# Second experts: W1 and W3 kept whole in SBUF and copied into slots by ScalarE, W2 streamed per tile

## The chip, the cores and the metric

The kernel runs on one core of one Trainium2 chip. The metric is the device time of one execution, in microseconds (us).

## What is computed

A block of two layers acts on x, 2 x 1024 tokens of 256 values in fp32. Each layer adds a gated mixing step and a gated mixture of experts. Only the mixture of layer 1, the "second experts", is touched by the change; attention stands before it.

```python
x = x + tanh(g_xattn[1]) * attention(layernorm(x), context)      # 16 heads, 77 context keys + 1024
h = layernorm(x)
scores = sigmoid(h @ gate_w.T)                                   # 32 experts
top 4 of scores + e_bias per token; weights = their scores / sum of them
g = h @ w1[e]; u = h @ w3[e]                                     # 256 x 192 each
out += weight * ((silu(g) * u) @ w2[e])                          # 192 x 256
x = x + tanh(g_ffn[1]) * out
```

## The kernel before, in words

Each stage is a block of code that gives every engine its own list of instructions (`nc.Block`); all engines meet at the end of a block. Within one, they are ordered by semaphores alone. The stages of layer 1 are `combine_and_project`, `attend`, `project_and_score`, `route`, `experts1` and `combine1`.

`route` sorts the 2048 x 4 (token, expert) pairs by expert and pads them to `NT1` = 95 tiles of 128 rows; a tile has one expert, whose number stands in `e.expert`. `experts1` (L1070 to L1231) then runs over the 95 tiles:

- POOL (`move_tiles`, L896) gathers the 128 rows of a tile by an indirect DMA into one of four slots of `xg`. It needs the column of row numbers that DVE writes (`token_column`, L929).
- SP (`load`, L1103) reads the tile's expert number and loads that expert's W1 and W3, 192 KB each, into one of the four slots of `e.w13` (L1108), once gate and up of four tiles before are done. `store` (L1110) sends the result of the tile six before to `y`.
- TensorE turns the gathered rows (`turn_x`, L1137, two tiles ahead), computes gate and up with the slot's W1 and W3 as the weights that it loads (`gate_up`, L1145), and the product with W2 (`down`, L1155), which lies behind by two tiles. W2 of all 32 experts is in SBUF (`e.w2b`, 64 KB of each partition); `down` picks the tile's by the expert number that it loads into a register (L1150).
- ScalarE does both SiLUs (L1187, L1189), and then copies the turned rows of the tile two ahead from PSUM to SBUF (`copy_x`, L1181).
- DVE multiplies (L1217 to L1219), copies the result of the tile two before into `ysb` (L1205), which waits for the store that last used that slot (L1203), and writes the row numbers of a tile four ahead of the one last turned (L929).

The order within a tile on TensorE is `gate_up(j)`, `down(j - 2)`, `turn_x(j + 2)`. `tile_loop` (L93) writes the first five tiles out and loops over turns of four.

W2 is brought at the end of `attend`: SP, when it has moved the last row maxima of the last group (L1667), issues 16 DMAs (`load_w2`, L1552; four experts in two DMAs: rows 0 to 127 of W2 on 128 partitions, rows 128 to 191 on 64). The pad rows of `e.w2b` are set to zero by POOL early in `attend` (L1737). In `project_and_score` SP stores the 16 normalised tiles to `xn` (L2030), which the gathers read later.

The `arena` of 160 KB of each partition is shared by all stages. Bytes from `ATT0` = 77824 on belong to attention's buffers until `attend` ends.

## Time and profile before

| what | value |
|---|---|
| median of 3 runs | 1368.84 us |
| lowest, highest | 1366.23, 1368.93 us |
| the profiled execution's own time | 1366.11 us |
| its span | 1364.4 us |
| TensorE busy (share of the span) | 1131.3 us (83%) |
| weight loads (PEld) busy | 741.5 us (54%) |
| DVE, ScalarE, POOL busy | 756.2, 585.3, 337.4 us |
| all DMA | 172.77 MB, mean 127 GB/s |

The span goes from the first to the last instruction that the profile shows; 1.7 us of the execution lie outside it. Busy times overlap between engines and don't add up to the span. PE is matmul, PEld is TensorE's weight load, which runs beside it; a name with q (SPq) is an engine's sequencer. "<-" in brackets names what ended an engine's idle time. L numbers are lines of the kernel before.

### The profile page before, as it was taken

Reading aid. Unit: us, or ns where it says so; the run is one execution under the profiler, and the core shown is the slowest. Engines: PE = TensorE matmul, PEld = TensorE weight load, DVE = VectorE, ACT = ScalarE, POOL = GpSimd, SP = SyncE. Lnnn points to the kernel's source line nnn. Section 1 sums busy time; section 2 is a strip of 40 time slices with the busy share of each in tenths; the row PEclk is TensorE's granted clock in tenths of the full one; section 3 lists DMA queues with packets and bytes.
Section 4 is the critical chain, followed back from the end, with each engine's and each line's share of the span. In section 5 each row is a group of like instructions: output and inputs, shape, how many; then the busy total and the mean of one; then the engine's idle time right before and its main releaser. Section 6 shows DMA issues by size and latency. Waiting matters only on the chain. (4 is left out here: it accounts for less than half of the span.)

```text
span 1364.4 us, 24973 instructions
## 1 busy us (share of the span) xinstructions
PE 1131.3 (83%) x6984; PEld 741.5 (54%) x6986; DVE 756.2 (55%) x2072; ACT 585.3 (43%) x1394; POOL 337.4 (25%) x538
## 2 busy tenths in 40 slices
PE   4849999999957879999999999997547999999200
PEld 2749999999944412333333333324417999888200
DVE  6551222222236487888888888832594555555433
ACT  2631221222124406777777777785453333333000
POOL 2012222222211244111111101010003333333476
PEclk9959999999978958999999999999658999999755
DMA  5455555554523533213113123043107888899343
GB/s 165 141 192 194 190 171 178 188 185 169 177 73 95 113 95 49 34 17 50 27 24 50 20 31 50 1 112 86 51 1 224 259 259 258 258 263 254 110 131 119
DMA packets 139935, 172.77 MB, mean 127 GB/s; under 512 B 17574, under 2 KB 118944, under 8 KB 139738
## 3 DMA queue, kind: packets, MB, share of 16 engines
q1 hardware_dynamic: 126186, 138.75, 37.7%
q0 software_dynamic: 11376, 31.08, 7.6%
q10 hardware_dynamic: 2304, 2.10, 0.4%
q8 instruction: 34, 0.56, 0.2%
q14 instruction: 35, 0.29, 0.1%
HBM read 141.29 MB, written 30.38 MB: 126 GB/s over the span
## 5 line engine op out<-in xcount | busy, mean ns | idle before, releaser
L1932 DVE TENSOR_REDUCE arena<-ps 128x1 f32<-128x512 f32 x512 | 327.7, 682 | 60.9 <-PE ps L1773 57.5
L1903 ACT ACTIVATE arena<-ps 128x512 f32<-128x512 f32 (+1 forms) x576 | 301.8, 598 | 130.4 <-PE ps L1814 129.0
L1814 PE MATMUL ps<-arena 99*128 99x512 bf16 (+1 forms) x576 | 216.6, 388 | 3.1 <-ACT arena L1903 2.7
L1773 PE MATMUL ps<-arena 96*128 96x512 bf16 x512 | 206.0, 405 | 8.8 <-PEq L1349 6.1
L896 POOL DMA_INDIRECT xg<-xn,tcol x134 | 127.7, 953 | 335.7 <-DVE tcol L929 332.6
L1803 PE MATMUL ps<-arena 128*17 128x512 f32 (+1 forms) x1152 | 153.3, 604 | 2.1 <-ACT arena L1903 1.0
L1814 PEld LDWEIGHTS ps<-arena 99*128 99x128 bf16 (+1 forms) x576 | 57.1, 101 | 174.5 <-ACT arena L1903 136.1
L987 PEld LDWEIGHTS ps<-scratch,arena 128*128 128x128 f32 x1248 | 147.4, 194 | 3.6 <-issue 1.7
L987 PE MATMUL ps<-scratch,arena 128*128 128x128 f32 x1248 | 147.9, 278 | 1.1 <-ACT scratch L1018 1.1
L1145 PE MATMUL ps<-scratch,arena 128*128 128x128 f32 x1140 | 146.4, 279 | 1.7 <-DMA arena<-in_L_ffn_w 0.5
L1000 PE MATMUL ps<-arena,scratch 128*128 x624 | 141.0, 379 | 0.0
L1145 PEld LDWEIGHTS ps<-scratch,arena 128*128 128x128 f32 x1140 | 135.9, 193 | 5.6 <-issue 4.2
L1000 PEld LDWEIGHTS ps<-arena,scratch 128*128 128x128 f32 x624 | 115.8, 190 | 14.0
L1057 DVE TENSOR_SCALAR scratch<-ps,arena 128x128 f32<-128x128 f32 x156 | 43.9, 344 | 126.4 <-PE ps L987 126.4
L1018 ACT ACTIVATE scratch<-ps 128x256 f32<-128x256 f32 x39 | 14.9, 383 | 209.5 <-PE ps L978 209.5
L1155 PE MATMUL ps<-arena,scratch 128*128 (+1 forms) x380 | 97.9, 380 | 0.7 <-DVE ysb L1205 0.7
L1217 DVE TENSOR_TENSOR scratch<-ps,scratch 64x128 f32<-64x128 f32 x95 | 27.8, 293 | 109.2 <-PE ps L1155 104.2
L1773 PEld LDWEIGHTS ps<-arena 96*128 96x128 bf16 x512 | 51.4, 101 | 58.7 <-DVE arena L1932 26.3
L1721 POOL TENSOR_TENSOR scratch<-arena 128x64 f32<-128x64 f32 x64 | 18.7, 292 | 255.0 <-DVE arena L1951 246.5
L1181 ACT ACTIVATE scratch<-ps 128x256 f32<-128x256 f32 x95 | 36.4, 383 | 86.8 <-PE ps L1137 86.8
L1251 POOL DMA_INDIRECT arena<-y,slot_u x64 | 61.2, 957 | 36.4 <-issue 19.2
L1155 PEld LDWEIGHTS ps<-arena,scratch 128*128 128x128 f32 (+1 forms) x380 | 65.3, 192 | 6.0 <-issue 1.1
(306 smaller groups left out, 1262.9 us busy)
## 6 DMA issues: line engine op xcount, KB each, us to landing
arena<-in_L_ffn_W SPq DMA_DIRECT2D x47, 1024.0 KB, 5.0
arena<-in_L_ffn_w SPq DMA_DIRECT2D x190, 192.0 KB, 3.7
y<-ysb SPq DMA_DIRECT2D x95, 128.0 KB, 4.2
arena<-k_parts SPq DMA_DIRECT2D x48, 137.6 KB, 5.0
arena<-q_parts SPq DMA_DIRECT2D x96, 64.0 KB, 6.0
arena<-y SPq DMA_DIRECT2D x16, 256.0 KB, 5.5
arena<-in_L_ffn_w SPq DMA_DIRECT2D x8, 512.0 KB, 10.3
xg<-xn,tcol POOLq DMA_INDIRECT x134, 4.4
```

Source lines behind the costliest of these rows:

```text
L896: pool.indirect_dma_start(out=e.xg[:, r, :], out_offset=None, in_=e.xn[layer], in_offset=bass.IndirectOffsetOnAxis(ap=e.tcol[:, r:r + 1], ...
L987: ins = nc.tensor.matmul(chunk(r, n), w1[:, r % 2, k, n * P:(n + 1) * P], xT[:, r % 2, k, :], start=(k == 0), stop=(k == DK - 1))
L1000: last = nc.tensor.matmul(ps[:, YB + r % 2, 0:D], hT[:, r % 2, k, :], e.w2[:, ex, k, :], start=(k == 0), stop=(k == HK0 - 1))
L1057: v.tensor_scalar(hT[:, r % 2, k, :], chunk(r, k), e.b1T[:, bass.ds(ex * HK0 + k, 1)], 0.0, ALU.add, ALU.max).then_inc(high_ready, 1)
L1145: ins = nc.tensor.matmul(chunk(r, n), e.w13[:, r, k, n * P:(n + 1) * P], xT[:, r % 2, k, :], start=(k == 0), stop=(k == DK - 1))
L1155: last = nc.tensor.matmul(ps[:, YB + r % 2, 0:D], hT[0:rows, r % 2, k, :], e.w2b[0:rows, ex, k, :], start=(k == 0), stop=(k == 1))
L1251: pool.indirect_dma_start(out=yg[:, i, k, :], out_offset=None, in_=e.y[1], in_offset=bass.IndirectOffsetOnAxis(ap=e.slot_u[:, i, k:k + 1], ...
L1773: nc.tensor.matmul(ps[:, MAXB + pos % NMAXB, :], e.q_aug[u][0:QROWS, c, h, t * P:(t + 1) * P], e.k_aug[u][0:QROWS, h, CL + k * HB:CL + (k ...
L1803: ins = nc.tensor.matmul(ps[h * 32:h * 32 + HD + 1, AB, :], e.v_g[u][0:rows, mt, h, :], e.prob[s % 2][0:rows, h, :], start=(mt == 0), stop ...
L1814: nc.tensor.matmul(ps[0:rows, SB + n % NSB, :], e.k_aug[u][0:AROWS, h, k0:k0 + rows], e.q_aug[u][0:AROWS, c, h, :], start=True, stop=True) ...
L1903: nc.scalar.activation(e.prob[s % 2][0:rows, h, :], ps[0:rows, SB + (s * GH + h) % NSB, :], ACT.Exp).then_inc(p_ready, 1)
L1932: v.tensor_reduce(e.mx[:, c, h, t, k:k + 1], ps[:, MAXB + pos % NMAXB, :], AX.X, ALU.max).then_inc(max_done, 1)
```

## The change

W2_1 and W13_1 change roles. W1 and W3 of all 32 experts (3072 bytes of each partition per expert) lie in SBUF whole, at the arena's start. Of these, 25 experts fit below `ATT0` and are loaded by SP at the end of `attend` in 50 DMAs of 192 KB; the other 7 are loaded by SP at the start of `project_and_score`, 14 DMAs, ahead of the stores to `xn`. In `experts1` ScalarE reads the tile's expert number and copies that expert's 768 fp32 values of each partition from the whole array into one of four slots (`bring`), and `gate_up` reads the slot. SP streams W2 per tile instead, into four slots (`e.w2r`), in two DMAs of 128 KB and 64 KB; each waits for the `down` of four tiles before. `down` waits for its W2 and no longer loads the expert number. The zeroing of the pad rows moves from POOL in `attend` to DVE at the start of `experts1`. The number of matmuls, their shapes and their order stay.

```diff
--- before.py
+++ after.py
@@ -51,9 +51,9 @@
 RAW0 = 2 * DK * H0 * 4
 ARENA0_END = W2_0 + E0 * HK0 * D * 4
 W13_BYTES = DK * 2 * I1 * 4
-W2_1 = 0
-W13_1 = W2_1 + E1 * 2 * D * 4
-W2_TURN = 4
+W13_1 = 0
+W13_RING = W13_1 + E1 * W13_BYTES
+W2_1 = W13_RING + RING1 * W13_BYTES
 ARENA = 163840
 ZN_AT = 32768
 YG0 = 32768
@@ -61,7 +61,8 @@
 LOGITS_AT = 3 * 4 * D * 4
 TOP = ARENA - (DK * D + D + DK * E1) * 4
 LOGITS1_AT = TOP - NTILE * E1 * 4
-ATT0 = W13_1 + RING1 * W13_BYTES
+ATT0 = 77824
+W13_EARLY = (ATT0 - W13_1) // W13_BYTES
 IA, IB = P, I1 - P
 IB_PAD = 96
 
@@ -134,7 +135,7 @@
         return e.used[-1]
 
     e.sem = new_semaphore
-    e.w0_in, e.w2_in = (ctx.enter_context(nc.semaphore(n)) for n in ("w0_in", "w2_in"))
+    e.w0_in, e.w13_in = (ctx.enter_context(nc.semaphore(n)) for n in ("w0_in", "w13_in"))
     e.x = sb("x_resident", [P, NTILE, D])
     e.arena = sb("arena", [P, ARENA // 4])
     e.scr = sb("scratch", [P, NTILE * D])
@@ -197,8 +198,9 @@
     e.w1 = carve(W1_0, [2, DK, H0])
     e.w2 = carve(W2_0, [E0, HK0, D])
 
-    e.w2b = carve(W2_1, [E1, 2, D])
-    e.w13 = carve(W13_1, [RING1, DK, 2 * I1])
+    e.w13 = carve(W13_1, [E1, DK * 2 * I1])
+    e.w13r = carve(W13_RING, [RING1, DK, 2 * I1])
+    e.w2r = carve(W2_1, [RING1, 2, D])
 
     e.raw = Memory()
     e.raw.wqkv = carve(RAW0, [6, D])
@@ -1071,8 +1073,8 @@
 
     nc, ps, sem = e.nc, e.ps, e.sem
     gathered = [sem(f"e1_gathered{r}") for r in range(RING1)]
-    w13_in = [sem(f"e1_w13_in{r}") for r in range(RING1)]
-    x_turned, xT_ready = sem("e1_x_turned"), sem("e1_xT_ready")
+    w2_in = [sem(f"e1_w2_in{r}") for r in range(RING1)]
+    x_turned, xT_ready, w13_ready = sem("e1_x_turned"), sem("e1_xT_ready"), sem("e1_w13_ready")
     gu_raw, silu_ready, h_ready = sem("e1_gu_raw"), sem("e1_silu_ready"), sem("e1_h_ready")
     y_raw, y_ready, tcol_ready = sem("e1_y_raw"), sem("e1_y_ready"), sem("e1_tcol_ready")
     y_stored = [sem(f"e1_y_stored{r}") for r in range(RING1)]
@@ -1103,9 +1105,10 @@
             def load(j, r):
                 ex = sp.value_load(e.expert[0:1, bass.ds(j, 1)], min_val=0, max_val=E1 - 1)
                 if at_least(j, RING1):
-                    sp.wait_ge(gu_raw, (j - RING1) * 2 + 2)
-                for at, name in ((0, "L1_ffn_w1"), (I1, "L1_ffn_w3")):
-                    sp.dma_start(e.w13[:, r, :, at:at + I1], e.a[name][bass.ds(ex, 1)].rearrange("e (k p) i -> p (e k) i", p=P)).then_inc(w13_in[r], 16)
+                    sp.wait_ge(y_raw, j - RING1 + 1)
+                w = e.a["L1_ffn_w2"][bass.ds(ex, 1)]
+                sp.dma_start(e.w2r[0:IA, r, 0, :], w[:, 0:IA].rearrange("e p d -> p (e d)")).then_inc(w2_in[r], 16)
+                sp.dma_start(e.w2r[0:IB, r, 1, :], w[:, IA:I1].rearrange("e p d -> p (e d)")).then_inc(w2_in[r], 16)
 
             def store(j, r):
                 sp.wait_ge(y_ready, j + 1)
@@ -1138,31 +1141,29 @@
                 last.then_inc(x_turned, 1)
 
             def gate_up(j, r, turn):
-                pe.wait_ge(w13_in[r], turn * 32 + 32)
+                pe.wait_ge(w13_ready, j + 1)
                 pe.wait_ge(xT_ready, j + 1)
                 for n in range(3):
                     for k in range(DK):
-                        ins = nc.tensor.matmul(chunk(r, n), e.w13[:, r, k, n * P:(n + 1) * P], xT[:, r % 2, k, :], start=(k == 0), stop=(k == DK - 1))
+                        ins = nc.tensor.matmul(chunk(r, n), e.w13r[:, r, k, n * P:(n + 1) * P], xT[:, r % 2, k, :], start=(k == 0), stop=(k == DK - 1))
                     if n != 1:
                         ins.then_inc(gu_raw, 1)
 
-            def down(j, r):
-                ex = pe.value_load(e.expert[0:1, bass.ds(j, 1)], min_val=0, max_val=E1 - 1)
+            def down(j, r, turn):
                 if at_least(j, 2):
                     pe.wait_ge(y_ready, j - 1)
                 pe.wait_ge(h_ready, j + 1)
+                pe.wait_ge(w2_in[r], turn * 32 + 32)
                 for k, rows in enumerate((IA, IB_PAD)):
-                    last = nc.tensor.matmul(ps[:, YB + r % 2, 0:D], hT[0:rows, r % 2, k, :], e.w2b[0:rows, ex, k, :], start=(k == 0), stop=(k == 1))
+                    last = nc.tensor.matmul(ps[:, YB + r % 2, 0:D], hT[0:rows, r % 2, k, :], e.w2r[0:rows, r, k, :], start=(k == 0), stop=(k == 1))
                 last.then_inc(y_raw, 1)
 
             def body(j, r, turn, first, last):
                 if at_least(j, 2):
                     pe.wait_ge(h_ready, j - 1)
                 gate_up(j, r, turn)
-                if isinstance(j, int) and j == 2:
-                    pe.wait_ge(e.w2_in, 32 * (E1 // W2_TURN))
                 if at_least(j, 2):
-                    down(j - 2, (r - 2) % RING1)
+                    down(j - 2, (r - 2) % RING1, turn if r >= 2 else turn - 1)
                 if before(j, NT1 - 2):
                     turn_x(j + 2, (r + 2) % RING1, turn + (r + 2) // RING1)
 
@@ -1170,7 +1171,7 @@
                 turn_x(j, j, 0)
             tile_loop(pe, NT1, RING1, body)
             for j in (NT1 - 2, NT1 - 1):
-                down(j, j % RING1)
+                down(j, j % RING1, j // RING1)
 
         @block.scalar
         def _(act):
@@ -1179,6 +1180,12 @@
                 if at_least(j, 2):
                     act.wait_ge(gu_raw, (j - 2) * 2 + 2)
                 nc.scalar.activation(xT[:, r % 2].rearrange("p k t -> p (k t)"), ps[:, XB + r % 2, 0:D], ACT.Copy).then_inc(xT_ready, 1)
+
+            def bring(j, r):
+                ex = act.value_load(e.expert[0:1, bass.ds(j, 1)], min_val=0, max_val=E1 - 1)
+                if at_least(j, RING1):
+                    act.wait_ge(gu_raw, (j - RING1) * 2 + 2)
+                nc.scalar.activation(e.w13r[:, r].rearrange("p k i -> p (k i)"), e.w13[:, ex, :], ACT.Copy).then_inc(w13_ready, 1)
 
             def body(j, r, turn, first, last):
                 if at_least(j, 2):
@@ -1189,8 +1196,11 @@
                 nc.scalar.activation(silu[0:IB, r % 2, 1, :], chunk(r, 1)[0:IB], ACT.Silu).then_inc(silu_ready, 1)
                 if before(j, NT1 - 2):
                     copy_x(j + 2, (r + 2) % RING1)
-
+                    bring(j + 2, (r + 2) % RING1)
+
+            act.wait_ge(e.w13_in, 32 * E1)
             for j in range(2):
+                bring(j, j)
                 copy_x(j, j)
             tile_loop(act, NT1, RING1, body)
 
@@ -1225,6 +1235,7 @@
             for j in range(RING1):
                 token_column(e, dve, j, j, tcol_ready)
             v.memset(hT[IB:IB_PAD, :, 1, :], 0.0)
+            v.memset(e.w2r[IB:IB_PAD, :, 1, :], 0.0)
             next_column(0, 0)
             tile_loop(dve, NT1, RING1, body)
             for j in (NT1 - 2, NT1 - 1):
@@ -1549,10 +1560,9 @@
         sp.dma_start(e.q_aug[u][n * HD:(n + 1) * HD, 1, :, :], qv[cq, gg, :, :, bass.ds(b * S + HB, HB)]).then_inc(e.q2_loaded[u], 16)
 
 
-def load_w2(e, eng, ex):
-    w = e.a["L1_ffn_w2"][ex:ex + W2_TURN]
-    eng.dma_start(e.w2b[0:IA, ex:ex + W2_TURN, 0, :], w[:, 0:IA].rearrange("e p d -> p e d")).then_inc(e.w2_in, 16)
-    eng.dma_start(e.w2b[0:IB, ex:ex + W2_TURN, 1, :], w[:, IA:I1].rearrange("e p d -> p e d")).then_inc(e.w2_in, 16)
+def load_w13(e, eng, ex):
+    for at, name in ((0, "L1_ffn_w1"), (I1, "L1_ffn_w3")):
+        eng.dma_start(e.w13[:, ex].rearrange("p (k i) -> p k i", k=DK)[:, :, at:at + I1], e.a[name][ex].rearrange("(k p) i -> p k i", p=P)).then_inc(e.w13_in, 16)
 
 
 STEPS = 2 * MT
@@ -1580,7 +1590,7 @@
     rows_max, neg_ready, negT_ready = sem("at_rows_max"), sem("at_neg_ready"), sem("at_negT_ready")
     step, carrier = sem("at_step"), sem("at_carrier")
     s_raw, p_ready, pv_done = sem("at_s_raw"), sem("at_p_ready"), sem("at_pv_done")
-    bias_added, pad_set = sem("at_bias_added"), sem("at_pad_set")
+    bias_added = sem("at_bias_added")
     half_out, half_inverted, half_done = (sem("at_half_" + n) for n in ("out", "inverted", "done"))
     MAXB, NMAXB, SB, NSB, AB, MB = 0, 3, 3, 3, 6, 7
     PARTS = len(QB)
@@ -1681,8 +1691,8 @@
                     maxima(g + 1, 1 - u, 0)
 
             groups(sp, body)
-            for ex in range(0, E1, W2_TURN):
-                load_w2(e, sp, ex)
+            for ex in range(W13_EARLY):
+                load_w13(e, sp, ex)
 
         @block.gpsimd
         def _(pool):
@@ -1734,8 +1744,6 @@
                 last = g_.tensor_tensor(e.x[:, i, :], e.x[:, i, :], e.bproj, ALU.add)
             last.then_inc(bias_added, 1)
             pool.wait_ge(bias_added, 1)
-            g_.memset(e.w2b[IB:IB_PAD, :, 1, :], 0.0).then_inc(pad_set, 1)
-            pool.wait_ge(pad_set, 1)
 
             def body(g, u, first, last):
                 if not last:
@@ -2025,6 +2033,8 @@
     with nc.Block() as block:
         @block.sync
         def _(sp):
+            for ex in range(W13_EARLY, E1):
+                load_w13(e, sp, ex)
             for i in range(NTILE):
                 sp.wait_ge(zn_ready, i + 1)
                 sp.dma_start(e.xn[1][i * P:(i + 1) * P, :], zn[:, i, :]).then_inc(zn_stored, 16)
```

## Rows read from the trace of the kernel before

**Rows 1.** Stretches of 30 us (its first line names the columns).

```profile
core 0: us, PE busy (x) PEld busy (x) DVE busy (x) ACT busy (x) POOL busy (x), PEclk, DMA share, GB/s
...
1050.00:1080.00 30.00, 30.00 (x222) 28.00 (x221) 16.25 (x60) 11.44 (x37) 10.95 (x12) 1.00 0.88 256
...
1200.00:1230.00 30.00, 29.40 (x213) 26.62 (x212) 15.65 (x59) 10.80 (x35) 11.20 (x12) 1.00 0.91 265
```

**Rows 2.** Timeline of one steady tile: start us, us, engine, line, what.

```profile
1152.85 0.89 SPq L1108 DMA_DIRECT2D arena<-in_L_ffn_w  x2
1152.88 0.38 PE L1137 MATMUL ps<-ident,xg 128*128 128x128 f32 x2
1152.91 0.94 POOL L896 DMA_INDIRECT xg<-xn,tcol  x1 [1.89 <-DVE tcol L929]
...
1153.10 1.50 PE L1145 MATMUL ps<-scratch,arena 128*128 128x128 f32 x12
...
1153.30 0.38 ACT L1181 ACTIVATE scratch<-ps 128x256 f32<-128x256 f32 x1 [0.82 <-PE ps L1137]
...
1154.64 0.27 ACT L1189 ACTIVATE scratch<-ps 64x128 f32<-64x128 f32 x1 [0.62 <-PE ps L1145]
...
1155.53 0.66 PE L1145 MATMUL ps<-scratch,arena 128*128 128x128 f32 x4
1155.58 0.29 DVE L1217 TENSOR_TENSOR scratch<-ps,scratch 64x128 f32<-64x128 f32 x1 [1.02 <-PE ps L1155]
```

**Rows 3.** Timeline of the second experts, its start and its last turned tile.

```profile
1029.46 0.15 DVE L929 COPY tcol<-token_u 128x1 uint32<-128x1 uint32 x1 [4.82 <-PE ps L1137]
...
1030.41 0.69 PE L1137 MATMUL ps<-ident,xg 128*128 128x128 f32 x2 [0.98 <-DMA xg<-xn,tcol]
...
1265.45 0.44 PE L1137 MATMUL ps<-ident,xg 128*128 128x128 f32 x2 [0.46 <-DMA xg<-xn,tcol]
```

**Rows 4.** Waits, 1033 to 1276 us: who waited for whom, us, times, longest.

```profile
PEld ps L1137 <- DMA xg<-xn,tcol: 4.5, 7, 1.4
PEld ps L1145 <- issue: 4.2, 13, 0.6
```

**Rows 5.** DMA issues, 1060 to 1260 us: KB each, median us to landing.

```profile
y<-ysb SPq DMA_DIRECT2D x79, 128.0 KB, 4.3
xg<-xn,tcol POOLq DMA_INDIRECT x80, 4.5
```

**Rows 6.** DMA of the first experts, 80 to 380 us.

```profile
DMA packets 15544, 53.08 MB, mean 177 GB/s; under 512 B 1871, under 2 KB 3023, under 8 KB 15407
...
xg<-xn,tcol POOLq DMA_INDIRECT x39, 3.4
```

**Rows 7.** ScalarE: line 741, and the timeline behind a loaded register.

```profile
L741 ACT ACTIVATE arena<-arena x1: 629/629/629, 977.5 to 977.5; 128x512 f32<-128x512 f32 x1
...
253.32 1.14 ACT L1028 ACTIVATE scratch<-ps,arena 128x128 f32<-128x128 f32 x4 [0.50 <-issue]
```

**Rows 8.** SP's DMA issues in attend, timeline, and that block's closing drain.

```profile
903.89 0.58 SPq L1554 DMA_DIRECT2D arena<-in_L_ffn_w  x1
...
923.45 2.29 SPq L1555 DMA_DIRECT2D arena<-in_L_ffn_w  x1
949.13 10.18 SPq L2030 DMA_DIRECT2D xn<-scratch  x7
...
L1660 POOLq DRAIN  x1: 386/386/386, 937.5 to 937.5; - x1
```

**Rows 9.** DMA queue of SP: 900 to 940 us, then 1024 to 1040 us.

```profile
q1 hardware_dynamic: 6496, 6.30, 72.0%
...
q1 hardware_dynamic: 3333, 2.41, 52.6%
```

**Rows 10.** Timeline of POOL at the start of attend.

```profile
517.73 6.92 POOL L1737 MEMSET arena<- 32x8192 f32 x1
...
535.31 0.26 POOL L1710 TENSOR_SCALAR arena<-arena 128x16 f32<-128x16 f32 x1 [7.15 <-DVE arena L1944]
```

## The prediction

> **What bounds the kernel now.** I first read the page's slices for the stretch that the change touches, the second experts, then a table by stretches of 30 us [rows 1]. There TensorE is busy for 98 to 100% at full clock, its weight loads for 89 to 93%, the DMA engines for 88 to 91% at some 260 GB/s, ScalarE for little over a third. Two things are near their limit, so I went on to the timeline of a steady tile [rows 2]: gate and up start at 1153.10 and again at 1155.53, a period of 2.43 us, in which one weight load follows another without a gap. That is TensorE's own rate, and the change leaves its matmuls alone. Were every tile like this, DMA would cost nothing. So I compared with the whole stretch: tile 1 is turned at 1030.41, the last at 1265.45 [rows 3], 93 periods in 235.04 us, 2.527 us each. **The excess is 93 x 0.097 = 9.0 us.** The waits name it [rows 4]: weight loads stood idle 4.5 us for gathered rows, and 4.2 us ahead of gate and up for what the profile calls issue, in 13 places; this kernel's only other wait there is that for the tile's W1 and W3. Both are DMAs that come a little late.
>
> **Why gathers are late, and what relieves them.** In a steady tile POOL starts a gather at 1152.91, as a tile is turned; its own tile is turned two periods after that, 4.83 us later [rows 2]. The median gather lands after 4.5 us here [rows 5], so the slow part of them misses. In the first experts, at 177 GB/s, it lands after 3.4 us [rows 6]. A tile moves 384 KB of weights, a gather and a store of 128 KB each. With W2 (192 KB) in place of W1 and W3 it moves 448 KB rather than 640 KB, in 2.43 us 189 GB/s, near the rate of the first experts. I take their latency: 1.4 us to spare. Bounds: the 4.5 us of today (no gain) and 3.4 us with no stall left (9.0 us). Since single gathers will still be late, I leave 0.7 us. Gain: **8.3 us**. The wait of gate and up for W1 and W3 goes from DMA to ScalarE, below.
>
> **What is added to ScalarE.** Per tile: a register load with its checks, and a copy of 128x768 fp32 within SBUF. The nearest copy is 128x512 fp32 from arena to arena, 0.63 us; a 128x256 from PSUM takes 0.38 [rows 7, 2], so 256 more cost some 0.21 to 0.25 us, and the copy 0.84 to 0.88 us. The register load is seen in the first experts, in the same order of work: there line 1028 follows the copy of the turned rows and a load of the expert number, and starts after 0.50 us of issue [rows 7]. Hence in the steady tile: copy of turned rows 1153.30 to 1153.68, copy of weights 1154.18 to about 1155.02. Its tile's gate and up start at 1155.53 [rows 2], so 0.5 us is left. ScalarE's whole round is 0.38 + 0.50 + 0.84 + two SiLUs of 0.27 = 2.26 us of 2.43. The SiLU of the next tile waits behind the copy: the second one, now at 1154.64, comes at about 1155.3 and ends before 1155.58, when DVE starts on its product after waiting for `down` [rows 2]. The cover for all of this is TensorE's 2.43 us. I cost it at 0.2 us for the first tiles, which have no `down` and a shorter period. If a copy took over 0.17 us more than I think, ScalarE would set the period.
>
> **SP in the second experts.** Two DMAs per tile before and after, 0.89 us of issue at 1152.85 [rows 2]. The load's wait moves to `down` of four tiles before, and the store of the tile six before is queued behind it. So that store leaves about 1.0 us after a `down` ends and lands 4.3 us later at today's latency [rows 5], 5.3 us after. DVE wants its slot two periods and the three products (0.9 us) after that `down`, 5.8 us after. It holds by 0.5 us today and by more with lighter traffic; if it failed, DVE's copy, then the row numbers queued behind it, then the gather would be late. Cost 0. W2 is asked for at `down` of four tiles before, four periods (9.7 us) ahead of its use: 0.
>
> **The start.** The zeroing of four slots' pad rows on DVE is hidden: DVE idles 4.82 us there until the first rows are turned [rows 3]. The first gathers compete with 0.8 MB of W2 rather than 1.6 MB, so they may land up to 0.9 us earlier: 0.5 us gained. POOL's zeroing of 6.92 us leaves `attend`, but POOL idles 7.15 us after it until 535.31 [rows 10], so it gains 0. The register load on TensorE's queue is hidden behind weight loads: 0.
>
> **The loads moved ahead.** SP issues the W2 DMAs from 903.89 to 925.74 [rows 8], and POOL reaches the block's end at 937.5: 11.8 us to spare. Now SP has 50 DMAs with 25 x 512 = 12,800 packets of 768 B instead of 6144 of 1 KB. Two rows price a packet of SP's queue [rows 9]: in 900 to 940 us 72.0% of 16 x 40 us over 6496 packets is 71 ns; in 1024 to 1040 us 52.6% of 16 x 16 us over 3333 is 40 ns, and these are mostly the very transfers that now move, W1 and W3, same shape, same source. I take 40 ns: 12,800 x 40 / 16 = 32 us, all landed at about 937, and SP done with issuing some us before that, since the queue holds what the engines have not taken (its last DMA before, issued at 923.45, was in the queue after 925.74). It waits for nobody. Cost 0. At 71 ns it costs 18 us (below).
>
> The Trainium skill, "SBUF — State Buffer", section "Door 1: The DMA port swizzle", says that a transfer reaches only as many of 16 ports as its partitions map to, and partitions 0 to 63 map to eight. Half of the W2 DMAs have 64 partitions, those of W1 and W3 all 128; by this rule 71 ns belongs to W2 and not to the loads that come. The sum is the same without it.
>
> The last 14 DMAs stand ahead of the `xn` stores on SP. 14 x 0.45 us of issue from 938 end at 944, landed by about 947; the first store leaves at 949.13 [rows 8]. Cost 0.
>
> **Sum.** -8.3 - 0.5 + 0.2 = -8.6 us. It is made against the profiled execution, 1366.11 us, 2.7 us below the median of 1368.84. From the median: **1360.2 us**.
>
> **Rivals.**
> *SP holds the end of `attend` (slower).* All engines wait for the slowest queue at the block's end. SP's issue is throttled to what the engines take. At 71 ns a packet, the first 6144 go in 21.85 us as now and the other 6656 at 4.44 ns each in 29.5 us: SP is done at 955.3 rather than 937.5, +17.8 us, 1378 us in all. It decides above some 49 ns: about 11,000 packets, the rest still queued, in the 33.6 us up to 937.5. At 53 ns (71 scaled to 768 B) it costs 3 us: 1363. For it: attention's own rows were the ones with 71 ns. Against: the same transfers at 40 ns. 0.06 for the first, 0.12 for the second.
> The Trainium skill, "DMA: Bandwidth & Descriptors", section "Bandwidth", speaks against the smaller DMAs: batch to 1 MiB or more; alone, 64 KB reaches 138 GB/s there. By that figure, an estimate, 9.8 MB would take 71 us and hold the block's end by over 25 us; the trace has 260 GB/s with DMAs of 128 to 192 KB, so it does not agree for queued ones.
> *ScalarE sets the period.* Were the copy 1.1 us or more, the round would be 2.52 us: +0.09 x 95 = 8.6 us, which gives everything back: 1368.8, and 9.5 us more per further 0.1 us. For it: only 0.17 us of slack, and register steps that the page doesn't count as busy. Against: the rows for both its parts. 0.12.
> *Gathers stay late.* If their 4.5 us is the gather's own and not the traffic's, only the waits for W1 and W3 go (4.2 us at most, perhaps 1): 1365 to 1368. Against: 3.4 us in the first experts. 0.10.
> The forecast has 0.60.
>
> **How the numbers follow.** About 0.2%, 2.7 us, is what a measurement of this kernel can tell from no change. Faster by more: the forecast, the small hold of `attend` and a part of the two last rivals, 0.76. Slower: the full hold and a ScalarE copy of 1.15 us or more, 0.12. Between: 0.12. The range goes down to 1355 (all 9.0 and 0.9 us gained and the profiled execution's 2.7 us lower level, with 1 us to spare) and up to 1369, which takes in the small hold, late gathers and the ScalarE round of 2.52 us; the full hold is left out.
>
> **What would show it.** Right: periods of 2.43 us nearly throughout, 93 of them in about 227 us; no wait of weight loads for gathered rows over 1 us in sum; gathers landing in about 3.4 us and 190 GB/s; ScalarE's copy 0.84 us and ending half a us ahead of gate and up; the drain of SP at the end of `attend` before POOL's; `xn` stores at the same distance from the block's start. Wrong: weight loads idle for ScalarE's copy in most tiles; TensorE's first work of `project_and_score` released by SP; DVE's copy into `ysb` waiting for stores.

## The result, and the profile after

The median went from 1368.84 us (five runs, 1366.23 to 1371.49) to **1378.84 us** (five runs, 1376.61 to 1381.63): 1.0078 of before, with a 95% interval of 1.0055 to 1.0100. The forecast was 1360.2 us, so the change costs 10.0 us where 8.6 were to be gained. The profiled execution took 1381.63 us with a span of 1379.9 us, 15.5 us over the span of before. It is the slowest of its five, and that of before (1366.11 us) is faster than all its other runs, so that 5.5 of the 15.5 us come from which executions were profiled.

I start where the forecast has its sum, at the turned tiles. Timeline of TensorE in after, tile 1 and the last tile (start us, us, engine, line, what):

```profile
1032.38 0.69 PE L1140 MATMUL ps<-ident,xg 128*128 128x128 f32 x2 [0.75 <-DMA xg<-xn,tcol]
...
1279.79 0.44 PE L1140 MATMUL ps<-ident,xg 128*128 128x128 f32 x2
```

That is 247.41 us for 93 periods, 2.660 us each, where [rows 3] gave 235.04 us and 2.527. So **12.4 of the 15.5 us lie in the second experts**. The other 3.1 us are the sum of four steps: 1.8 us more up to the end of `attend`, 1.2 from there to TensorE's last instruction of `route`, 1.2 behind the last turned tile, and 1.0 less between `route` and the turn of tile 1. The first two are not shown to be the change's: in the kernels of the experiments below, `attend` ends between 937.5 and 940.3 us, whichever loads it issues, and `route` is done 85.4 or 86.6 to 86.7 us later. Stretches of 30 us in after, answering to [rows 1]:

```profile
core 0: us, PE busy (x) PEld busy (x) DVE busy (x) ACT busy (x) POOL busy (x), PEclk, DMA share, GB/s
1050.00:1080.00 30.00, 30.00 (x224) 27.95 (x223) 15.78 (x58) 19.05 (x51) 11.37 (x12) 1.00 0.59 171
1200.00:1230.00 30.00, 28.21 (x196) 24.11 (x194) 14.91 (x55) 17.00 (x44) 10.42 (x11) 1.00 0.57 169
```

In the first stretch TensorE runs as before, with nothing between its matmuls. Later it does 196 matmuls in 30 us rather than 213. DMA is not what it lacks: the share fell from 0.88 to 0.59. Nor is it ScalarE, busy for 17 to 19 of 30 us. No engine of the table is near its limit in the second stretch, so the next view is that of the waits, 1036 to 1290 us of after:

```profile
POOL xg L898 <- DVE tcol L931: 157.5, 90, 3.7
DVE ysb L1215 <- DMA y<-ysb: 99.0, 81, 2.1
...
PEld ps L1140 <- DMA xg<-xn,tcol: 20.3, 46, 1.2
...
PEld ps L1148 <- issue: 5.3, 14, 0.5
```

The second row is new: DVE stands 99 us in sum for stores of `y`. The third is what TensorE feels of it, and the fourth, 5.3 us of "issue" ahead of gate and up, is taken up in "Why the prediction was wrong". DVE's copy into `ysb` waits for a slot that a store has not yet emptied; the row numbers are queued behind it on DVE; POOL's gather waits for them; and TensorE waits for the gather. It is the chain that the prediction named under "SP in the second experts", where it set it against 0.5 us of slack with stores that land after 4.3 us. But the stores land faster than before, not slower. DMA issues in after, 1060 to 1260 us, answering to [rows 5]:

```profile
DMA packets 30932, 34.14 MB, mean 171 GB/s; under 512 B 4765, under 2 KB 28546, under 8 KB 30932
...
y<-ysb SPq DMA_DIRECT2D x74, 128.0 KB, 2.2
```

2.2 us from issue to landing. So the stores are issued late, and SP is who issues them. What does SP wait for? Its own waits, first in before (1036 to 1262 us), then in after (1036 to 1290 us):

```profile
SPq L1112 <- DVE ysb L1205: 0.4, 1, 0.4
```

```profile
SPq L1110 <- PE ps L1158: 7.4, 3, 6.3
SPq L1115 <- DVE ysb L1215: 1.4, 3, 0.9
```

**SP waits for nothing, in either kernel.** The 7.4 us in after lie ahead of its first store. A queue that waits for nothing over 90 tiles has no time left, and the profile's page has no column that would say so, because it doesn't count such instructions as busy. Stores of `y` on SP, timeline, before and then after:

```profile
1050.29 0.37 SPq L1112 DMA_DIRECT2D y<-ysb  x1
...
1260.04 0.37 SPq L1112 DMA_DIRECT2D y<-ysb  x1
```

```profile
1050.72 0.37 SPq L1115 DMA_DIRECT2D y<-ysb  x1
...
1260.07 0.42 SPq L1115 DMA_DIRECT2D y<-ysb  x1
```

In before 83 rounds lie between the two stores, 2.527 us each, the period of TensorE. In after there are 78, **2.684 us each**. Other first and last stores of the same stretch give 2.53 to 2.54 and 2.68 to 2.70 us, so the third decimal is no evidence. Where a round goes, from the views of SP's lines: duration in ns, lowest/median/highest, of one instruction of each kind; first before, then after.

```profile
L1104 SPq FUSED_REGOPS  x161: 46/152/177, 1024.2 to 1260.9; - x161
L1104 SPq TENSOR_LOAD <-expert x95: 262/270/739, 1023.9 to 1260.6; - x95
...
L1108 SPq DMA_DIRECT2D arena<-in_L_ffn_w x190: 372/394/1495, 1024.7 to 1261.8; - x190
L1108 SPq FUSED_REGOPS  x95: 37/43/48, 1024.5 to 1261.2; - x95
...
L1112 SPq DMA_DIRECT2D y<-ysb x95: 332/368/1505, 1039.2 to 1273.7; - x95
L1112 SPq FUSED_REGOPS  x88: 46/46/51, 1039.1 to 1259.9; - x88
```

```profile
L1106 SPq FUSED_REGOPS  x161: 51/155/171, 1027.2 to 1282.6; - x161
L1106 SPq TENSOR_LOAD <-expert x95: 262/270/662, 1026.9 to 1282.3; - x95
...
L1110 SPq FUSED_REGOPS  x95: 37/43/43, 1027.5 to 1282.9; - x95
...
L1110 SPq DMA_DIRECT2D arena<-in_L_ffn_w x95: 337/341/357, 1027.7 to 1283.0; - x95
...
L1111 SPq FUSED_REGOPS  x95: 37/43/47, 1028.1 to 1283.4; - x95
...
L1111 SPq DMA_DIRECT2D arena<-in_L_ffn_w x95: 479/503/1390, 1028.2 to 1283.9; - x95
...
L1115 SPq DMA_DIRECT2D y<-ysb x95: 332/418/562, 1047.2 to 1288.6; - x95
L1115 SPq FUSED_REGOPS  x88: 51/51/56, 1047.1 to 1281.5; - x88
```

With three register moves of 29 ns and a check of 18 ns in each kernel, one of each kind, taken at its median, adds up to 1.772 us before (270 + 152 + 18, 43 + 2 x 29 + 2 x 394, 46 + 29 + 368) and 1.929 us after (270 + 155 + 18, 43 + 29 + 341, 43 + 29 + 503, 51 + 29 + 418). The difference is 0.157 us, as is that of the two rounds; that they agree to the thousandth is luck. Its parts: the second DMA, of 64 partitions, takes 503 ns where one of W1 or W3 takes 394 (+0.109); the first takes 341 (-0.053); the second DMA has register steps of its own (+0.043); the store's issue takes 418 ns rather than 368 (+0.050, and 0.008 in register steps, of which 0.003 are the load's). The change has two DMAs for two, fewer bytes, and a longer round.

The rest of the round, 0.75 us, is not in this sum of medians. Summed over all rows of SP in those rounds, the loop's own and the slower ones among the shown included, SP's instructions take 1.95 us a round before and 2.09 after. The last 0.57 and 0.60 us are in no row: waits that were already fulfilled and steps between instructions. Timeline of SP in after, which shows a turn of the loop:

```profile
1149.79 0.42 SPq L1115 DMA_DIRECT2D y<-ysb  x1
1151.07 0.34 SPq L1110 DMA_DIRECT2D arena<-in_L_ffn_w  x1
1151.61 0.50 SPq L1111 DMA_DIRECT2D arena<-in_L_ffn_w  x1
1152.30 0.43 SPq L1115 DMA_DIRECT2D y<-ysb  x1
1154.11 0.34 SPq L1110 DMA_DIRECT2D arena<-in_L_ffn_w  x1
```

From the end of one store to the next load's first DMA it takes 0.86 us (1150.21 to 1151.07), from the next store's end 1.38 us (1152.73 to 1154.11). This longer gap comes once in four tiles, which is once in a turn of the loop. The rounds of after are three of 2.50 to 2.59 us and one of 2.9 to 3.3 (3.14 in the median); those of before three of 2.38 to 2.6 and one of 2.7 to 3.2 (2.90).

The Trainium skill, "Perfetto Trace Analysis", section "What "DMA-bound" means", says that a kernel can be bound by the sequencer that issues DMAs, and that one sees it by a track of solid DMA slices. The first half is what happened here. The second would have missed it: DMA slices fill 0.341 + 0.503 + 0.418 = 1.26 us of a round of 2.68 in after, 47%. The section "Sequencer-only Instruction (DRAIN, etc)" of the same page says that waits on semaphores and their propagation are outside the reported window; the 0.57 to 0.60 us without a row agree with that, though no run here splits them.

### The profile page after: what moved, and what is told of

It is laid out like the page before. It is cut to its first block and busy times, and to the rows that moved or that the text cites. A ratio compares the mean times of both kernels' runs of the same rounds, so it can differ in the third digit from the quotient of the medians.

```text
span 1379.9 us, 25229 instructions
## 1 busy us (share of the span) xinstructions
PE 1142.5 (83%) x6985; PEld 740.8 (54%) x6986; DVE 757.5 (55%) x2073; ACT 645.7 (47%) x1489; POOL 330.7 (24%) x537
## 5 line engine op out<-in xcount | busy, mean ns | idle before, releaser
L1020 ACT ACTIVATE scratch<-ps 128x256 f32<-128x256 f32 x39 | 15.0, 384 | 209.9 <-PE ps L980 209.9
L1158 PE MATMUL ps<-arena,scratch 128*128 128x256 f32 (+1 forms) x380 | 98.5, 382 | 1.5 <-DVE ysb L1215 1.3
L1188 ACT ACTIVATE arena<-arena 128x768 f32 x95 | 80.1, 843 | 41.4 <-PE ps L1148 34.2
L1215 DVE COPY ysb<-ps 128x256 f32<-128x256 f32 x95 | 40.4, 425 | 100.2 <-DMA y<-ysb 99.0
```

What stands on the lines that cost most here:

```text
L1158: last = nc.tensor.matmul(ps[:, YB + r % 2, 0:D], hT[0:rows, r % 2, k, :], e.w2r[0:rows, r, k, :], start=(k == 0), stop=(k == 1))
L1188: nc.scalar.activation(e.w13r[:, r].rearrange("p k i -> p (k i)"), e.w13[:, ex, :], ACT.Copy).then_inc(w13_ready, 1)
```

## The experiments

**Theory S:** SP's own instructions set the period, 2.53 us before and 2.68 after, and TensorE's 2.43 comes back once SP's round is shorter. **Rivals:** ScalarE's copy sets it (C); the order of load and store on SP does, with a store held behind a load that waits for `down` (O); the DMA traffic does (D), which the prediction held for the kernel before. All stretches below go from the turn of tile 1 to that of the last tile, in each kernel's profile; before has 235.0 us, after 247.4.

| run | stretch, us | period, us | time, us | before beside it, us | ratio (95%) |
|---|---|---|---|---|---|
| e1 after, SP written out | 227.1 | 2.442 | 1356.66 | 1368.02 | 0.9903 (0.9886 to 0.9919) |
| e2 before, SP written out | 235.8 | 2.535 | 1365.47 | 1368.02 | 0.9974 (0.9959 to 0.9988) |
| e3 after, store ahead of load | 240.2 | 2.583 | 1373.70 | 1368.02 | 1.0041 (1.0026 to 1.0057) |
| e4 after, a third of the copy | 245.1 | 2.636 | 1380.19 | 1368.02 | one run |
| e5 before, one more register load | 284.2 | 3.056 | 1417.75 | 1364.73 | one run |
| e6 after, second DMA on 128 partitions | 228.3 | 2.454 | 1361.62 | 1364.73 | 0.9978 (0.9969 to 0.9988) |
| e7 before written out, without W3 | 226.8 | 2.438 | 1357.56 | 1364.73 | 0.9943 (0.9926 to 0.9959) |
| e8 after, one W2 DMA | 226.9 | 2.439 | 1361.15 | 1364.73 | one run |
| e9 after, W2's rest at partition 64 | 257.9 | 2.773 | 1393.68 | 1368.07 | 1.0183 (1.0169 to 1.0197) |
| e10 as e1, another chip | 226.9 | 2.440 | 1360.60 | 1368.07 | 0.9945 (0.9932 to 0.9959) |
| e11 e9 with SP written out | 257.8 | 2.772 | 1390.43 | 1368.07 | 1.0166 (1.0150 to 1.0181) |
| e12 e1 with one more register load | 274.3 | 2.950 | 1409.53 | 1368.07 | one run |
| e13 as e9, full-height weights | 230.1 | 2.474 | 1365.32 | 1368.60 | 0.9977 (0.9964 to 0.9990) |

### SP's list written out (e1, e2, e10)

In both kernels the loop on SP's queue becomes 89 bodies one after another; nothing else is touched. It takes the loop's turn and the register steps of computed addresses off SP.

```diff
-            turns = (NT1 - LAG_Y) // RING1
-            with sp.Fori(0, turns) as t:
-                for u in range(RING1):
-                    body(t * RING1 + (LAG_Y + u), (LAG_Y + u) % RING1, None, False, False)
-            for j in range(LAG_Y + turns * RING1, NT1):
+            for j in range(LAG_Y, NT1):
                 body(j, j % RING1, None, False, False)
```

> The changed kernel, with SP's list for the second experts written out for all 95 tiles in place of a loop over turns of four: wait values, slots and addresses of the stores become constants and the branch goes; the loads, stores, waits and their order stay. Theory S (SP's own instructions, 2.69 us a tile, set the period): SP's round falls by 0.3 us or more to under 2.43, the mean period falls from 2.65 to about 2.45 us, and the kernel gains about 95 x 0.2 = 19 us, to some 1360 us; DVE's waits for stores (99 us) nearly vanish. Theory O (the store is late because it is queued behind a load that waits for a down product): DVE's waits for stores stay, and the time stays within 5 us of 1379. Theory C (ScalarE's copy of 0.84 us is in the way): no change.

> The kernel before, with SP's list for the second experts written out in the same way. Theory S: SP's round of 2.53 us was the bound already, so its mean period falls from 2.53 towards 2.43, up to 9 us gained; what is left over 2.43 is late DMA. Theory G (in the kernel before only DMA traffic made gathers and weights late, as I predicted): no change, 1369 us, and the waits for gathered rows stay at 4.5 us.

**Measured.** e1: 1356.66 us, 0.9903 of before. Timeline of TensorE in e1, tile 1 and the last tile:

```profile
1030.77 0.69 PE L1136 MATMUL ps<-ident,xg 128*128 128x128 f32 x2 [0.88 <-DMA xg<-xn,tcol]
...
1257.89 0.38 PE L1136 MATMUL ps<-ident,xg 128*128 128x128 f32 x2
```

Its stretch is 227.1 us, the "93 of them in about 227 us" of the prediction. SP now waits; its waits in e1, 1036 to 1262 us:

```profile
SPq L1115 <- DVE ysb L1211: 7.9, 28, 1.0
SPq L1110 <- PE ps L1154: 7.7, 3, 6.4
```

The waits of the other engines in e1 have neither DVE's row for stores (99.0 us in after) nor one of TensorE for gathers. e2: 1365.47 us, 0.9974 of before, while its stretch shows nothing gained (its profile is of an execution of 1369.32 us, at the upper end of its ten runs). SP waits 40.0 us there for results that are not ready, so it isn't the bound, and yet a period is 2.535 us. The waits of SP and of TensorE in e2, same stretch:

```profile
SPq L1112 <- DVE ysb L1201: 40.0, 78, 1.2
...
PEld ps L1133 <- DMA xg<-xn,tcol: 6.2, 18, 1.0
...
PEld ps L1141 <- issue: 4.8, 13, 0.5
```

**What follows.** In after SP's round is the whole of the loss in the second experts: the same data moved by the same DMAs, with SP's queue freed of its loop, gains what was forecast. In before two limits lie together near 2.53 us: SP's round, and late DMAs behind it. Taking SP away from before leaves the second almost untouched.

The same kernel on another chip, with which the later runs are compared:

> The changed kernel with SP's list written out, once more for its interval: 1356.7 us within 2, period 2.44 us, ratio to the kernel before 0.990 to 0.995.

**Measured.** 1360.60 us, above the 1356.7 within 2 that I expected, and 0.9945 of before, inside the expected ratio; the period is 2.440 us again. The gain in time differs between the chips, 11.4 and 7.5 us, by more than the intervals allow; the stretch of the second experts doesn't (227.1 and 226.9 us). So what differs lies outside it: in the two profiles `attend` ends at 937.5 and 939.5 us, a difference that kernels with either set of loads show. No run here says what sets it.

### The order on SP, and ScalarE's copy (e3, e4)

e3 puts the store ahead of the load:

```diff
             def body(j, r, turn, first, last):
-                load(j, r)
                 if at_least(j, LAG_Y):
                     store(j - LAG_Y, (r - LAG_Y) % RING1)
+                load(j, r)
```

> The changed kernel, with each tile's store issued ahead of the load instead of behind it, so that no store is queued behind a wait for a down product. Theory S: SP's round is the same 2.69 us, so the period stays 2.65 and the time 1379 within 3 us; the late wait may move from the slot of the result to another place. Theory O: DVE's waits for stores vanish and the period falls to about 2.45 us, 1360 us.

e4 lets ScalarE copy 256 of the 768 values of each partition:

```diff
-                nc.scalar.activation(e.w13r[:, r].rearrange("p k i -> p (k i)"), e.w13[:, ex, :], ACT.Copy).then_inc(w13_ready, 1)
+                nc.scalar.activation(e.w13r[:, r].rearrange("p k i -> p (k i)")[:, 0:256], e.w13[:, ex, 0:256], ACT.Copy).then_inc(w13_ready, 1)
```

> The changed kernel, with ScalarE copying only the first 256 of the 768 values of each partition, so that gate and up work on wrong weights: part of the copy is left out. ScalarE is relieved of some 0.42 us a tile. Theory C: the period falls by 0.1 to 0.2 us, 10 to 19 us in all. Theories S and O: no change, 1379 us within 3.

**Measured.** e3: 1373.70 us, 5 us under after and outside what either theory expected, 2.637 us a round of SP over 80 rounds, still without a wait behind its first tiles. The order is worth more than I had put it at. Part of it is S's own: the queue stays full, and its round is 0.05 us shorter. The rest, I take it, is who gets the lateness, which no run shows by itself: DVE's wait for stores fell to 45.2 us, and `down` waits for W2 in its place (7.6 us, and 8.0 us of "issue"). Rival O in its own words, a store held behind a load that waits for `down`, falls by the waits of after: in steady tiles SP's load waits for nothing. e4, whose gate and up work on weights that are in part wrong: 1380.19 us, 1.3 us over the median of after, 2.3 us less in the stretch, with SP's round at 2.68 us and DVE's wait for stores still at 82.9 us (to 1262 us; 89.4 in after). A copy takes 0.417 us there. **C falls**: with two thirds of the copy gone the loss stays, but for those 2.3 us.

### Doses on SP's queue (e5, e12)

One register load per tile whose value nobody uses, in before and in e1's kernel:

```diff
             def load(j, r):
+                sp.value_load(e.expert[0:1, bass.ds(j, 1)], min_val=0, max_val=E1 - 1)
                 ex = sp.value_load(e.expert[0:1, bass.ds(j, 1)], min_val=0, max_val=E1 - 1)
```

> The kernel before, with the expert number loaded into a register once more per tile on SP, to no use: some 0.27 us of load, 0.15 and 0.02 us of check and the gaps between them, about 0.5 us in all; no DMA is added. Theory S: SP's round of 2.53 us has no slack, so it becomes 3.0 us and the time rises by 95 x 0.5 = 47 us, to some 1415 us. If TensorE or DMA were the bound before (2.43 us of TensorE, DMA as it is), most of the 0.5 us would still show, since 2.53 + 0.5 is over 2.43, but only if SP is full already; with SP as idle as I took it to be, nothing would show.

> The changed kernel with SP's list written out, and with the expert number loaded once more per tile on SP, to no use (about 0.5 us). Written out, SP's instructions take some 2.38 us of 2.43, of which 0.58 us is the issue of the store, which was 0.42 us in the loop. If that is SP's own fixed cost, the round becomes 2.85 us and the time rises by 95 x 0.42 = 40 us to some 1397. If part of the issue time is a wait for room in the queue, that SP spends either way, the rise is smaller, down to 0.25 us a tile, 24 us, to 1380.

**Measured.** e5: 1417.75 us, as expected under S; the stretch grew by 49.1 us, 0.528 us per tile. The added load with its steps shows 0.274 + 0.152 + 0.018 = 0.444 us in the view of its line. So the whole of it came through, and 0.084 us that no row has. SP has no slack in the kernel before. e12: 47.2 us over e1's stretch, 0.508 us per tile, and again all of it, in a kernel that gave TensorE 2.44 us. I had left some room there, and 1409.53 us is above my range of 1380 to 1397. SP's round in e1's kernel is thus just under TensorE's period (most rounds take 2.38 us), and no more: the store's issue takes 583 ns there (418 in after), which eats a part of what the written-out list saves.

### W2's second DMA (e6, e8)

e6 moves rows 64 to 191 to 128 partitions in place of rows 128 to 191 to 64: twice the bytes. e8 leaves the DMA out.

```diff
-                sp.dma_start(e.w2r[0:IB, r, 1, :], w[:, IA:I1].rearrange("e p d -> p (e d)")).then_inc(w2_in[r], 16)
+                sp.dma_start(e.w2r[0:P, r, 1, :], w[:, I1 - P:I1].rearrange("e p d -> p (e d)")).then_inc(w2_in[r], 16)
...
-            v.memset(e.w2r[IB:IB_PAD, :, 1, :], 0.0)
```

```diff
-                sp.dma_start(e.w2r[0:IB, r, 1, :], w[:, IA:I1].rearrange("e p d -> p (e d)")).then_inc(w2_in[r], 16)
...
-                pe.wait_ge(w2_in[r], turn * 32 + 32)
+                pe.wait_ge(w2_in[r], turn * 16 + 16)
```

> The changed kernel, with the second W2 DMA of a tile taking 128 rows (64 to 191) onto 128 partitions instead of 64 rows onto 64: the second half of the down product gets wrong rows. More bytes (512 KB a tile for 448), same number of DMAs. In the changed kernel SP spends 0.50 us on issuing the 64-partition DMA and 0.34 us on the 128-partition one. Theory S with the 64-partition shape as the dear part: the issue falls to 0.34 us, SP's round from 2.69 to about 2.52 us, the time by 10 to 15 us, to 1364 to 1369 us, in spite of the added bytes. If bytes in flight set SP's issue time, it stays at 0.50 us or more and the time at 1379 or above.

> The changed kernel, loop as it is, with the second W2 DMA of a tile left out (rows 128 to 191 of W2 are never loaded). SP saves 0.50 us of issue and about 0.12 us of register steps: its round would be 2.07 us, under TensorE's 2.43. Theory S: the period is 2.43 to 2.45 us and the time 1357 us within 3, as with the list written out. Theory C or O: still over 1370 us.

**Measured.** The view of line 1111 in e6:

```profile
L1111 SPq DMA_DIRECT2D arena<-in_L_ffn_w x95: 332/333/358, 1028.8 to 1262.5; - x95
```

**The DMA with twice the bytes is issued in 0.333 us rather than 0.503.** SP's round falls to 2.438 us over 86 rounds, though the loop is kept, TensorE's period to 2.454 us, and the time to 1361.62 us, 0.9978 of before. I had expected a round of about 2.52 us and 1364 to 1369 us; the time is below that, on a chip where before takes 4 us less than in the result. The round falls by 0.25 us, of which this DMA is 0.170; the store's issue is at 0.35 to 0.36 us rather than 0.42, another 0.06. In e8 the period is 2.439 us, as expected, and SP now waits:

```profile
SPq L1110 <- PE ps L1157: 54.2, 72, 9.2
```

So taking the instruction away gives TensorE little more than making it short (2.439 and 2.454 us a tile). The time of e8's one run, 1361.15 us, is 1 us above my range of 1357 within 3; in its profile `attend` ends 2.7 us later than in e1's.

### What traffic is worth (e7)

Before with SP's list written out, and W3 not loaded:

```diff
-                for at, name in ((0, "L1_ffn_w1"), (I1, "L1_ffn_w3")):
+                for at, name in ((0, "L1_ffn_w1"),):
...
-                pe.wait_ge(w13_in[r], turn * 32 + 32)
+                pe.wait_ge(w13_in[r], turn * 16 + 16)
```

> The kernel before with SP's list written out, and with W3 not loaded: up works on what lies in the slots. The traffic of a tile falls from 640 to 448 KB, that of the changed kernel, without ScalarE's copy and without W1 and W3 ahead of time. Theory: in the kernel before two limits lay close together, SP's round and late gathers under 260 GB/s; with SP written out the second is left (6.2 us of waits for gathered rows, period 2.535). If it is the traffic, gathers now land in about 3.4 us, the period is 2.43 to 2.45 us as in the changed kernel written out, and the time 1357 us within 3. If gathers are late for another reason, the period stays at 2.53 and the time at 1365.

**Measured.** 1357.56 us, 0.9943 of before. Timeline of TensorE in e7, tile 1 and the last tile:

```profile
1033.58 0.69 PE L1133 MATMUL ps<-ident,xg 128*128 128x128 f32 x2 [0.99 <-DMA xg<-xn,tcol]
...
1260.34 0.38 PE L1133 MATMUL ps<-ident,xg 128*128 128x128 f32 x2
```

The period is 2.438 us; W1 lands in 2.5 us and `y` in 2.0. e2 and e7 both have SP written out and waiting; what differs is one DMA of 192 KB per tile, and that takes 2.535 down to 2.438 us. So D is right as a second limit of before, worth 9 us of the stretch, and it is this one that the change removes.

### W2 on all 128 partitions, with the whole computation (e9, e11, e13)

e6 shows the price of 64 partitions but multiplies other rows than the layer wants. e9 keeps the short DMA and puts the rest in order: rows 64 to 191 fill the slot's 128 partitions, of which 64 to 127 hold the wanted rows; the second half of the SiLU and of the product moves to partitions 64 to 127, and `down` takes its second part from there. e11 is e9 with SP's list written out.

```diff
...
-                for k, rows in enumerate((IA, IB_PAD)):
-                    last = nc.tensor.matmul(ps[:, YB + r % 2, 0:D], hT[0:rows, r % 2, k, :], e.w2r[0:rows, r, k, :], start=(k == 0), stop=(k == 1))
+                for k, first in enumerate((0, P - IB)):
+                    last = nc.tensor.matmul(ps[:, YB + r % 2, 0:D], hT[first:P, r % 2, k, :], e.w2r[first:P, r, k, :], start=(k == 0), stop=(k == 1))
...
-                nc.scalar.activation(silu[0:IB, r % 2, 1, :], chunk(r, 1)[0:IB], ACT.Silu).then_inc(silu_ready, 1)
+                nc.scalar.activation(silu[IB:P, r % 2, 1, :], chunk(r, 1)[0:IB], ACT.Silu).then_inc(silu_ready, 1)
...
```

> The changed kernel, loop as it is, whole computation: the second W2 DMA takes rows 64 to 191 onto 128 partitions, so that rows 128 to 191 lie on partitions 64 to 127, and the second half of the SiLU, of the products and of the down product is kept on those partitions (64 rows, no pad). As in the run with the same DMA and wrong rows, SP's issue of it is 0.33 us instead of 0.50, its round some 2.44 us, and the time 1361 us within 3, at least 12 us under the changed kernel and some 3 us under the kernel before. If moving half the work to the upper partitions costs TensorE, DVE or ScalarE anything, the steady period is over 2.43 us.

> Both: SP's list written out and W2's second DMA on 128 partitions. SP gets 0.15 us more to spare, but TensorE's 2.43 us is reached already, so theory S expects nothing more: 1356 to 1359 us. The added bytes (512 KB a tile for 448) could make single gathers late and cost 1 or 2 us.

**Measured.** 1393.68 and 1390.43 us, where I had expected 1361 within 3 and 1356 to 1359. Both are slower than after, by the same 10.4 us of the stretch. SP's list makes no difference to the period (2.773, 2.772), so this is not SP. Timeline of a steady tile in e9:

```profile
1152.37 0.29 PEld L1158 LDWEIGHTS ps<-arena,scratch 64*128 64x128 f32 x2 [0.33 <-issue]
...
1152.99 0.20 PEld L1140 LDWEIGHTS ps<-ident,xg 128*128 128x128 f32 x2 [0.33 <-issue]
```

Two gaps of 0.33 us in every tile, one ahead of the weight load of 64 rows and one behind it, in which TensorE waits for nothing that the profile shows. The matmuls in flight cover a part of them; what is left is 2.77 less 2.43, 0.34 us a tile. e13 keeps all of e9 but lets the second part of `down` take 128 rows, with zeros in the lower 64 rows of `hT`:

```diff
-                for k, first in enumerate((0, P - IB)):
-                    last = nc.tensor.matmul(ps[:, YB + r % 2, 0:D], hT[first:P, r % 2, k, :], e.w2r[first:P, r, k, :], start=(k == 0), stop=(k == 1))
+                for k in range(2):
+                    last = nc.tensor.matmul(ps[:, YB + r % 2, 0:D], hT[:, r % 2, k, :], e.w2r[:, r, k, :], start=(k == 0), stop=(k == 1))
...
+            v.memset(hT[0:P - IB, :, 1, :], 0.0)
```

> The changed kernel, loop as it is, whole computation: W2's second DMA takes rows 64 to 191 onto 128 partitions as in e9, but the second half of the down product takes all 128 partitions, with zeros in the SiLU product's lower 64, so that no matmul has its weights on partitions 64 to 127 alone. The SiLU and the product stay shifted to the upper partitions as in e9. In e9 the period was 2.77 us, with gaps of 0.33 us ahead of the 64-row weight load and ahead of the next one. If the gaps come from the weights on the upper 64 partitions alone: they vanish, SP's round of 2.44 us with its 0.33 us issue is left, and the time is 1361 us within 3. If they come from the shifted SiLU or product: the period stays at 2.77 us and the time at 1393.

**Measured.** 1365.32 us (twelve runs), 0.9977 of before, 1.3 us above the range that I expected; the stretch is 230.1 us. Timeline of TensorE's weight loads in e13, the four of `down` and the next:

```profile
1150.74 0.73 PEld L1158 LDWEIGHTS ps<-arena,scratch 128*128 128x128 f32 x4
1151.50 0.36 PEld L1140 LDWEIGHTS ps<-ident,xg 128*128 128x128 f32 x2
```

The gaps of 0.33 us are gone. So they belong to the weight load that takes 64 rows from partition 64 on, and not to the shifted SiLU and product. Whether the number of rows or the place does it was not tried; a load of 96 rows from partition 0 (before and after have it in every tile) shows no such gap. For 64 rows of zeros e13 is 28.4 us faster than e9 by the medians, and 13.5 us faster than after, with the loop kept. It doesn't reach e1: SP's mean round over 84 rounds is 2.486 us rather than the 2.44 that I expected, and DVE still waits 14.0 us for stores.

**The best version** of these is e1: the change, with SP's list written out. On two chips it was faster than before (0.9903 and 0.9945); beside after it was not run, but lies 22 and 18 us under its 1378.84 us.

## Why the prediction was wrong

**The step that failed** is "SP in the second experts", with its "Two DMAs per tile before and after, 0.89 us of issue" and "Cost 0". It counted a queue by its DMAs. SP's round is 2.53 us, of which the 0.89 us are a third, and the new round was never added up. It measured 2.684 us, 0.157 longer than before; against TensorE's 2.43 us, 0.25 us a tile are missing. The first 20 or so tiles run at 2.43 us, since SP enters its loop ahead; then the lead is used up. The price: 247.4 us for the stretch against the 227 forecast.

**The reading of the kernel before** was half right. "TensorE's own rate" and "the excess" of 9.0 us stand nearly: 93 periods of 2.43 are 226.0 us, and e1, e7, e8 and e10 all end at 226.8 to 227.1, so that 7.9 to 8.3 us of the 9.0 could be had. But "Both are DMAs that come a little late" asked only why they land late, not when they were asked for. e5 shows that SP had no time left, e2 that the traffic binds too: with SP freed it alone gives 2.535 us. That SP alone would give 2.53 is read from its missing waits; no run took the traffic away and left SP's round. The row that says so, 0.4 us of waits of SP over 90 tiles, was in the trace of before, and the prediction doesn't have it among its rows. It also took the 4.2 us of "issue" ahead of gate and up for waits for W1 and W3, as the only other wait there. In the code gate and up wait for the turned rows and the SiLU product too, and after, which loads no W1 or W3 there, has the same row with 5.3 us in 14 places; e1 and e7 have none. So this row is not shown to be those loads.

**Relief of the gathers, -8.3 us:** right in mechanism and in size, once SP is out of the way. DMA went from 256 GB/s to 186 in e1 (1050 to 1080 us; 190 forecast), gathers no longer hold TensorE there, and the stretch fell by 7.9 us (235.0 to 227.1). The forecast landing of a gather, 3.4 us, is not shown: the views of after, e1 and e7 give no time for it.

**ScalarE:** right. The view of line 1188 in after:

```profile
L1188 ACT ACTIVATE arena<-arena x95: 842/843/845, 1027.5 to 1281.1; 128x768 f32 x95
```

0.843 us against "0.84 to 0.88", and e4 shows that a copy half as long gives 2.3 us of the 20.3 that after lacks. In a steady tile of e1 the copy ends at 1092.14 and gate and up start at 1092.78, 0.64 us later, where the prediction left 0.5. The nearest rows [rows 7] carried it. The rival "ScalarE sets the period" is refuted in after, and in e1 too, where the full copy runs at a period of 2.442 us. The Trainium skill, "ScalarE: Activation LUTs", section "What ACT_TABLE_LOAD costs", has a rule for an activation with immediate scale and bias, 186 ns and 0.833 ns for each element of a partition. By it, an estimate, 768 take 826 ns; the trace agrees to 2%.

**The wait that the change adds** was named and priced by the wrong quantity. "It holds by 0.5 us" took landing at 4.3 us and a store issued as soon as the load's wait ends. Landing was 2.2 us, so the slack by this sum was 2.6 us. The store was late because SP got to it late. The place was right, DVE's copy into `ysb`, and my last line of what would show the prediction wrong names it; the cause that I would have read into it, a load holding the store, is not it: in steady tiles SP's load waits for nothing.

**The loads moved ahead** cost nothing, as forecast. Timeline of SP at the end of `attend` in after, its next stage, the drains that close the block, and SP's queue from 905 to 940 us (packets, MB, share of 16 engines' time):

```profile
905.71 41.22 SPq L1565 DMA_DIRECT2D arena<-in_L_ffn_w  x64
952.43 2.86 SPq L2040 DMA_DIRECT2D xn<-scratch  x3
...
L1670 SPq DRAIN  x1: 122/122/122, 934.6 to 934.6; - x1
...
L1670 POOLq DRAIN  x1: 386/386/386, 939.3 to 939.3; - x1
...
q1 hardware_dynamic: 13696, 9.85, 93.9%
```

SP reaches the end at 934.6 us and POOL at 939.3. The price of 40 ns a packet held: 93.9% of 16 x 35 us over 13,696 packets is 38 ns. I had put SP's issue at "some us before" 937; the rival "SP holds the end of `attend`" would need it behind POOL's. The 14 later DMAs end at 946.9, ahead of the first store at 952.43, which waits for data. That store stands 13.1 us behind POOL's drain, 11.6 in before; e2, e5 and e7, with the loads of before, have 13.2 too, so this is not the loads'. The zeroing on DVE (0.91 us at 1027.81, in DVE's idle time) cost nothing, as forecast. From TensorE's last instruction of `route` to the turn of tile 1 it took 7.48 us before and 6.43 after (7.2 to 7.6 and 6.2 to 6.8 in the other runs of either), so the start gained about 0.9 us rather than 0.5. "That gathers stay late" came true to the eye, 20.3 us in TensorE's waits, for a reason that the rival didn't have: they are issued late.

**The chances.** Faster had 0.76, and slower was given to two other mechanisms. The bound that was missing is that of an engine with no wait: I searched the profile's page for busy shares, and SP has none there.

## What to carry to other kernels

A queue that only issues DMAs can be the bound while every busy share looks harmless: look first at its waits, and if there are none, take its round from the first and last of one of its instructions and compare it with the period. When a change swaps DMAs, add up every instruction of the new round, register loads, address steps and the loop's turn included; a DMA of half the partitions and a third of the bytes can cost the queue more than the one it replaces. Such a queue with a lead hides the loss for many tiles, so read a late stretch and not only the first steady one; and where it is the bound, writing its loop out is a cheap thing to try (here 22 us of 1379).

## What was not expected of the hardware

- **Issue by shape.** On SP a DMA into 64 partitions (64 KB, 1 KB each) took 0.503 us to issue, into 128 partitions (128 KB, 1 KB each) 0.333 to 0.341, into 128 partitions of 2 x 768 B 0.394. Fewer partitions and fewer bytes took longer. What the sequencer does in that time no run shows.
- **A register load on SP** takes 0.27 us and 0.17 us of steps behind it (e5 and e12: 0.53 and 0.51 us per tile in all). The Trainium skill, "DMA: Bandwidth & Descriptors", section "Latency and other measured facts", gives about 600 ns as the floor of `tensor_load`; the rows have less than half of that as the median, and up to 0.74 us as the highest.
- **The loop's turn on SP.** One round in four, the one with the turn, is longer than the others by 0.5 us in the median in before and 0.6 in after (0.3 to 0.8). Written out, most rounds of e1 are 2.38 us and one in about 13 is 0.4 us longer, for which no row gives a reason.
- **A store's issue** took 0.418 us in after, 0.368 in before, 0.35 in e6 and 0.583 in e1, with the same shape. What it depends on stays open.
- **A weight load of 64 rows from partition 64 on** is not overlapped: 0.33 us ahead of it and 0.33 us behind it, 2.77 us a tile rather than 2.43 (e9, e11). With 128 rows, half of them zero, both gaps vanish (e13).
